# Ranking by one key in fp16 parts, weight maxima on TensorE, and four row buffers for the plain sums, in a one-core graph network kernel

## The reference

```python
h = jnp.maximum(_layernorm(x), 0.0)
x = x + gat_conv(relu(gat_conv(h, W1, ...)), W2, ...)   # layers 1, 2: attention over edges
h = jnp.maximum(_layernorm(x), 0.0)
x = x + gcn_conv(relu(gcn_conv(h, W3, ...)), W4, ...)   # layers 3, 4: plain normalised sums
```

## Time and profile before

| | |
|---|---|
| median of 3 runs | 2283.92 us (2281.28 to 2285.07) |
| the profiled execution | 2278.45 us, of which its span is 2276.7 us |
| busy, share of the span | PE 97%, PEld 63%, DVE 67%, ACT 41%, POOL 40% |
| mean granted clock of TensorE | 0.992 |
| DMA | 407.32 MB, 179 GB/s |

### The profile page before, as it was taken

How to read it: one execution, slowest core, us unless ns; L and a number is a source line. 1 busy time by engine, 2 the same in 40 slices (tenths; PEclk the granted TensorE clock), 3 DMA queues, 4 the chain that set the end, 5 groups by cost and what they waited for, 6 DMA issues and landing times.

```text
span 2276.7 us, 36746 instructions
## 1 busy us (share of the span) xinstructions
PE 2212.1 (97%) x13888; PEld 1428.2 (63%) x13888; DVE 1520.7 (67%) x3352; ACT 935.1 (41%) x1291; POOL 904.6 (40%) x1071
## 2 busy tenths in 40 slices
PE   6999999999999999999999999999999999999997
PEld 3666666666666666666666666666665666666664
DVE  6888885444577776334589999766555657885564
ACT  3333433333455445433454444433333333333442
...
GB/s 141 154 118 106 111 112 113 113 127 202 160 195 190 186 188 167 124 167 119 192 209 184 195 207 207 200 250 241 244 241 205 222 185 237 247 252 178 181 208 82
DMA packets 125668, 407.32 MB, mean 179 GB/s; under 512 B 21993, under 2 KB 22151, under 8 KB 125364
## 3 DMA queue, kind: packets, MB, share of 16 engines
...
## 4 chain that ended last, share of the span: by engine, by line
PE 80%; DVE 8%; POOL 4%; issue 4%; DMA 2%; ACT 2%; SPq 0%; POOLq 0%; ACTq 0%; DVEq 0%
PE ps_h L893 67%; PE ps_z L876 8%; DMA edge_mem<-rows,pos_dst 2%; PE ps_e L960 1%; PE ps_e L961 1%; DVE z_lo L1106 1%; DVE bn L1054 1%; POOL out L604 1%; DVE edge_mem L1136 1%; DVE res L1125 1%; ACT row_out L782 1%; POOL edge_mem L599 1%; DVE res L1115 1%; POOL rstd L613 1%; PE ps_e L968 0%
## 5 line engine op out<-in xcount | busy, mean ns | idle before, releaser
L893 PE MATMUL ps_h<-w_hi,z_hi 128*128 128x384 f16 x3792 | 928.4, 327 | 0.4 <-DVE w_lo L1045 0.4
L893 PE MATMUL ps_h<-w_lo,z_hi 128*128 128x384 f16 x3792 | 928.2, 327 | 0.0
L893 PE MATMUL ps_h<-w_hi,z_lo 128*128 128x384 f16 x3792 | 927.9, 326 | 0.0
L1106 DVE TENSOR_TENSOR z_lo<-ps_z,z_hi 128x768 f16<-128x768 f32 x316 | 301.7, 955 | 484.5 <-ACT z_hi L787 483.8
L893 PEld LDWEIGHTS ps_h<-w_lo,z_hi 128*128 128x128 f16 x3792 | 371.5, 98 | 246.4 <-issue 1.9
L893 PEld LDWEIGHTS ps_h<-w_hi,z_lo 128*128 128x128 f16 x3792 | 371.5, 98 | 246.0 <-issue 1.4
L893 PEld LDWEIGHTS ps_h<-w_hi,z_hi 128*128 128x128 f16 x3792 | 371.3, 98 | 223.6 <-issue 19.9
L782 ACT ACTIVATE row_out<-ps_h,grow 128x768 f32<-128x768 f32 x237 | 212.9, 898 | 637.7 <-PE ps_h L893 628.1
L876 PE MATMUL ps_z<-ident,z 128*128 128x128 f32 x1896 | 261.0, 274 | 24.8 <-ACT z L795 23.6
L611 POOL TENSOR_SCALAR veps<-mv 128x1 f32<-128x1 f32 x158 | 87.5, 554 | 457.2 <-DVE mv L1057 441.9
L787 ACT ACTIVATE z_hi<-ps_z 128x768 f16<-128x768 f32 x316 | 253.8, 803 | 15.4 <-PE ps_z L876 15.4
...
## 6 DMA issues: line engine op xcount, KB each, us to landing
...
```

The source lines that it names most:

```text
L893: last = nc.tensor.matmul(ps_h[s][:, a, 0:HALF], zp[s][:, c, :], wp[:, c, a * HALF:(a + 1) * HALF], start=(c == 0 and zp is z_hi and wp is ...
L1106: V.tensor_tensor(pair3(z_lo[t.slot]), psum_pair(ps_z), pair3(z_hi[t.slot]), ALU.subtract).then_inc(z_lo_ready, 1)
```

## The change

It touches five places.

- **Ranking by one key.** `row_key` holds (dst - NP/2) * 2560 + index, so that one compare with a sum (`is_lt`) per column takes the place of two passes over 128x2560. The one-hots and `sorts` are f16, and `sorts` holds four parts of 7 bits (dst low, dst high, src low, src high) of which `keep_ranks` makes the numbers again. A column stands in two of every three windows.
- **Weight maxima.** `all_max` is a TensorE product of ones with a diagonal of the maxima, and DVE takes the maximum of the row. For W1 it stands in window 0, for W2 to W4 in `side_step(0)` of the windows in `max_at`. The load of W1 is issued one window later, behind the load of the second tile's rows; DVE takes W1's maxima behind the second tile's statistics, and makes scale and lower halves of W1 ahead of the third tile's statistics.
- **Masks' rows.** The dst values are turned by one transpose behind `prefixes`, stored (`store_dst`) and loaded back to all 128 partitions by one broadcast DMA of 2 x 2560 values (`load_masks`). `mask_diag` and `mask_rows` are gone, and `mask_make` has two instructions for four.
- **Side products moved.** `prefixes`, `turn_positions` and `turn_meta` stand in `side_step(0)` of a later window; the DVE work between them is spread over more windows; the clearing product at the head of layer 2 is gone; `sqrt_degree` stands in layer 2.
- **Plain sums.** Layers 3 and 4 share `sum_rows`, `sum_carry` and `sum_mm` with four row buffers, filled three sums ahead; the first four are gathered in two windows. `plain_at` and `last_at` begin later and end at the same window as before.

```diff
-    RANKED = 2 + 2 * ET
-    ORDER = RANKED + 4
-    SCATTERED = ORDER + 20
-    ORDERED = SCATTERED + 4
-    EACH = -(-NT // 20)
+    assert NP * EP <= 2 ** 25
+    rank_at = {2 + (3 * c) // 2: c for c in range(EC)}
+    RANKED = max(rank_at) + 2
+    COUNTED = RANKED + 1
+    TURNED = COUNTED + 4
+    ORDER = TURNED + 4
+    EACH = 4
+    SCATTERED = ORDER + -(-NT // EACH)
+    ORDERED = SCATTERED + 5
+    MASKS = ORDER + 3
+    assert ORDERED + 8 < NT
...
-    plain_at = {begin["4"] + 2 + (8 * j) // 5: j for j in range(ET)}
-    last_at = {begin["5"] + 3 + (7 * j) // 5: j for j in range(ET)}
+    plain_at = {begin["4"] + 4 + (3 * j) // 2: j for j in range(ET)}
+    last_at = {begin["5"] + 4 + (27 * j) // 20: j for j in range(ET)}
...
+    max_at = {2: TURNED + 4, 3: ORDERED + 1, 4: begin["2m"] + 14}
...
+            def store_dst():
+                sp.wait_ge(dst_turned, 1)
+                sp.dma_start(dst_rows, rows_t[0:2 * ET, :]).then_inc(dst_stored, 16)
+            def load_masks():
+                sp.wait_ge(dst_stored, 16)
+                sp.dma_start(rank_mem[:, 0:2, :].rearrange("p a q -> p (a q)"),
+                             bass.AP(dst_rows.tensor, dst_rows.offset, [[0, P], [1, 2 * EP]])).then_inc(masks_loaded, 16)
...
-                if w == -3:
+                if w == -2:
...
+                if w == COUNTED + 1:
+                    store_dst()
+                if w == COUNTED + 3:
+                    load_masks()
+                if w == TURNED + 2:
...
+            def sum_rows(layer, j):
+                h = j + (layer - 1) * ET
                 if j >= 4:
-                    pool.wait_ge(edge_done, 3 * ET + 2 + (j - 3))
-                gather(last_src[j % 4], pos_src[:, j:j + 1], table[4][0:NP - PURE * P, :], last_in[j % 4])
-                gather(last_base[j % 4], pos_base[:, j:j + 1], base_rows, last_in[j % 4])
-            def first_last_rows():
+                    pool.wait_ge(edge_done, h - 1)
+                gather(last_src[j % 4], pos_src[:, j:j + 1], table[layer][0:NP - PURE * P, :], last_in[j % 4])
+                if layer == 3:
+                    gather(last_base[j % 4][:, 0:D], pos_dst[:, j:j + 1], table[3][0:NP - PURE * P, :], last_in[j % 4])
+                else:
+                    gather(last_base[j % 4], pos_base[:, j:j + 1], base_rows, last_in[j % 4])
...
+                for layer, at in ((3, plain_at), (4, last_at)):
+                    if w in at and 4 <= at[w] + 3 < ET:
+                        sum_rows(layer, at[w] + 3)
+                    for k in range(2):
+                        if w == min(at) - 2 + k:
+                            if k == 0:
+                                (plain_rows_free if layer == 3 else last_rows_free)()
+                            sum_rows(layer, 2 * k)
+                            sum_rows(layer, 2 * k + 1)
...
-            def all_max(layer):
-                pool.wait_ge(w_max, layer)
-                nc.gpsimd.partition_all_reduce(w_scale[:, layer - 1, 1:2], w_scale[:, layer - 1, 0:1], P, RMAX).then_inc(w_max_all, 1)
...
-                if w == ORDERED + 3:
+                if w == begin["2"] + 2:
...
-            def mask_rows(j):
-                pe.wait_ge(dst_diag, j + 1)
-                nc.tensor.matmul(mask_ps, ones[:, :], diag2[:, :, :].rearrange("p a q -> p (a q)"),
-                                 start=True, stop=True, skip_group_check=True).then_inc(mask_mm, 1)
...
+                    if k == 0:
+                        if w == COUNTED:
+                            prefixes()
+                        if w == TURNED:
+                            turn_positions()
+                        if w == ORDERED - 1:
+                            turn_meta()
+                        for layer, at in max_at.items():
+                            if w == at:
+                                all_max(layer)
...
-                if 2 <= w < RANKED and w % 2 == 1:
-                    rank_mm((w - 2) // 2)
+                if w - 1 in rank_at:
+                    rank_mm(rank_at[w - 1])
...
+            def all_max(layer):
+                pe.wait_ge(w_max, layer)
+                nc.tensor.matmul(w_max_ps, ones[:, :], w_diag, start=True, stop=True, skip_group_check=True).then_inc(w_max_all, 1)
...
-                if w == RANKED:
-                    prefixes()
-                if w == RANKED + 2:
-                    turn_positions()
-                if w == ORDERED:
-                    turn_meta()
-                if w == begin["2"]:
-                    clear_for_edges()
+                if w == 0:
+                    all_max(1)
...
-                    V.tensor_reduce(w_scale[:, layer - 1, 0:1], w_top[:, layer - 1, :], AX_X, ALU.max).then_inc(w_max, 1)
+                    step(V.tensor_reduce(w_scale[:, layer - 1, 0:1], w_top[:, layer - 1, :], AX_X, ALU.max))
+                    V.tensor_scalar(w_diag, ident[:, :], w_scale[:, layer - 1, 0:1], None, ALU.mult).then_inc(w_max, 1)
...
+                step(V.tensor_reduce(sc[:, 1:2], w_max_ps, AX_X, ALU.max))
...
-                V.scalar_tensor_tensor(row_cmp, row_iota, edge_id[:, col], row_dst, ALU.is_lt, ALU.subtract).then_inc(ranks_step, 1)
+                k = c * 4
+                V.tensor_scalar(row_cmp, row_key, e_f[:, 2, col], 0.0, ALU.is_lt, ALU.add, accum_out=e_rank[:, 0, 0:1]).then_inc(ranks_step, 1)
...
-                V.tensor_scalar(row_cmp, row_cmp, e_f[:, 2, col], 0.0, ALU.is_gt, ALU.add, accum_out=e_rank[:, 0, 0:1]).then_inc(ranks_step, 1)
...
-                V.tensor_scalar(sorts[:, slot, 0:ET], iota_c[:, 0:ET], e_rank[:, 1, 0:1], e_f[:, 0, col], ALU.is_equal, ALU.mult)
-                V.tensor_scalar(sorts[:, slot, ET:2 * ET], iota_c[:, 0:ET], e_rank[:, 1, 0:1], e_f[:, 1, col], ALU.is_equal, ALU.mult)
+                for n in range(4):
+                    V.tensor_scalar(sorts[:, slot, n * ET:(n + 1) * ET], iota_c[:, 0:ET], e_rank[:, 1, 0:1], e_f[:, 3 + n, col],
+                                    ALU.is_equal, ALU.mult)
...
-                V.tensor_scalar(e_arg[:, :], mask_ps[:, 0:P], dst_of[:, col], FAR, ALU.is_equal, ALU.mult).then_inc(mask_part, 1)
-                V.tensor_scalar(same_t[:, j, :], mask_ps[:, P:2 * P], dst_in[:, col], None, ALU.is_equal)
-                dve.wait_ge(mask_part, j + 1)
-                V.tensor_scalar(far_mask[:, j, :], e_arg[:, :], -FAR, None, ALU.add).then_inc(mask_ready, 1)
+                if j == 0:
+                    dve.wait_ge(masks_loaded, 16)
+                V.tensor_scalar(far_mask[:, j, :], far_mask[:, j, :], dst_of[:, col], -FAR, ALU.not_equal, ALU.mult)
+                V.tensor_scalar(same_t[:, j, :], same_t[:, j, :], dst_in[:, col], None, ALU.is_equal).then_inc(mask_ready, 1)
...
+                step(V.tensor_scalar(row_key, row_cmp.bitcast(I32), -float(NP // 2), float(EP), ALU.add, ALU.mult))
+                V.tensor_tensor(row_key, row_key, row_iota, ALU.add)
...
+                if w == -1:
+                    scale_w(1)
+                    for c in range(KC):
+                        low_w(1, c)
...
-                if w == RANKED + 1:
+                if w == COUNTED + 1:
+                    first_sums()
+                if w == COUNTED + 2:
+                    other_sums()
+                if w == COUNTED + 3:
                     node_positions()
-                if w == RANKED + 2:
-                    last_edges()
-                if w == RANKED + 3:
+                if w == TURNED + 1:
+                    keep_positions()
+                    last_edges(0, ET // 2)
+                if w == TURNED + 2:
+                    last_edges(ET // 2, ET)
```

192 lines of the change are left out of this document (84 added, 108 removed).

## The result

The changed kernel takes 2227.19 us (median of 4 executions, 2225.99 to 2231.59) beside 2284.49 us before (4 executions, 2281.28 to 2285.30): ratio 0.9755, 95% interval 0.9738 to 0.9772. The profiled executions are 2225.99 and 2278.45 us, with spans of 2224.1 and 2276.7 us. So the profiled pair differs by 52.5 us and the medians by 57.3.

A forecast was written before the change was run, and what follows sets the result against it. TensorE's work plus its waits was taken to bound the kernel. The terms summed to 47.7 us, 46.2 after 1.5 for new waits, giving 2232 from the profile or 2238 from the median; predicted 2237 us, range 2229 to 2251.

The forecast's parts named there:

- W2's reduction: Window of W2's maxima: TensorE's wait for z and matmuls at half clock behind it all go, 6.3 us.
- no column outgrew its window: Rival on DVE's ranking: columns too long to hide under TensorE; 16.5 us lost at 7.7 us each, 2254; chance 0.02.
- four buffers did help: Rival on layer 3's plain sums: four buffers do not help, all 9.2 us of waits stay, 2245 us; chance 0.12.
- the power at its new place: Rival: the moved power over the degrees holds up layer 2's edges, 6 to 12 us, 2246 us; chance 0.05.
- The clock's rival: Each new short wait brings a stretch at 1.2 GHz; three or four cost 6 to 8 us, 2244; chance 0.10.
- Two of my signs: Signs expected in the profile: `rank_mm` at 0.2 to 0.3 us a column; TensorE's carried-row waits under 3 us.
- plain sums of layer 3: 7.5 (bounds 4 and 9.2): Rows asked three sums ahead, not one, remove TensorE's carried-row waits: 7.5 us of 9.2, leaving 1.7.
- The offset of 5.5 us: Median of before lies 5.5 us above its profiled execution; 2232 from the profile, 2238 from the median.
- Products of a column: Ranking's products on TensorE, f16 with 198 columns: 0.63 to 0.23 us, twenty times, 8.0 us (bounds 5.0 and 11.0).
- The start: First product at 18.1 us instead of 28.94, less a 1.6 us wait and 0.8 for clock: 8.4 (bounds 6.5 and 9.2).
- Waits for z: 3.4: Two waits behind a busy GpSimd, the degrees' power and eight gathers in one window: 3.4 us (bounds 0 and 3.7).
- new short waits: Allowance for short new waits in denser windows: 1.5 us put back, taking the sum from 47.7 to 46.2 us.

The follow-up runs named there:

- run 2: Changed kernel with the rows of layer 3's plain sums asked one sum ahead instead of three, four buffers kept: 2246.29 us.
- run 7: Changed kernel with layer 3's plain sums 1.6 windows apart as before, instead of 1.5, rows still asked three sums ahead: 2226.81 us.
- run 3: Changed kernel with the four weight maxima reduced across partitions on GpSimd instead of TensorE: 2241.43 us.
- run 1: The kernel before, unchanged, profiled a second time: 2284.23 us, ratio to before 1.0001.
- run 9: The changed kernel, unchanged, profiled again: 2226.17 us, ratio 0.9748.
- run 4: Changed kernel with the ranking's one-hots and sorted values in f32 instead of f16: 2236.72 us.
- run 6: Changed kernel with the power over the degrees (`sqrt_degree`) back in layer 1: 2227.31 us.
- run 12: Changed kernel with carried-row copy ahead of z, norm factors ahead of gathers, and edge-weight transposes behind the next turn: 2224.71 us.
- run 14: Changed kernel with W3's load one piece a window, carried-row copy ahead of z, and norm factors ahead of gathers: 2223.77 us, ratio 0.9733.
- run 10: Changed kernel with ACT's copy of a sum's carried row ahead of its window's z instead of behind it: 2225.92 us.

## Why the prediction was wrong

**The bound and the mechanisms were right.** TensorE's work plus its waits is the time, and every edit acted where I had put it: DVE's column 5.20 us for 5.25, W2's reduction 6.3 us, the end of the ranking 4.6 for 4.5, the masks' products 8.7 for 8.6 ahead of new waits, the clearing 1.7 for 1.8, the first product at 17.5 for 18.1. The 6.3 us are those of the first profile; the second has 5.2 there. None of the rivals came: no column outgrew its window, four buffers did help (runs 2 and 7), the granted clock was 1.00 from 22 us to the last tiles, the power at its new place cost nothing. The clock's rival took each short wait for a stretch at 1.2 GHz; the three waits of 1.0 to 1.1 us in the last sums left the clock at 1.00. What the rule of the Trainium skill, VectorE: DVE Perf Modes, section Rules for kernel authors (reduce across partitions on GpSimd), would have kept, run 3 measured as 14.2 us slower. Two of my signs did not hold: `rank_mm` takes 0.1 us a column where I had 0.2 to 0.3, and the waits for the carried row are 3.3 us, over the 3 I allowed, in layer 4 and not in layer 3.

**The step that failed is the term "plain sums of layer 3: 7.5 (bounds 4 and 9.2)".** I took the sum of idle times in the earlier trace rows as all that the waits could give back. By turns the same seven waits are 11.0 us in that profile and 14.4 in the second (run 1). A wait costs its idle time and about 0.25 us to get going again (runs 1 and 2), and where the clock falls behind it 1.9 us in all (run 1). I also left 1.7 us of waits, as layer 4 had; none came. The term is 3.5 us too small in the first pair of profiles and 7.1 in the second (14.6), and its upper bound was no bound. It alone takes the time out of the range: my upper bounds add up to 53.5 us, the first pair gained 52.8 and the second 57.6, with 5.4 us above the bound in the plain sums and 1.6 at the start.

**The offset of 5.5 us between the profiled execution and the median of before was carried over as a constant.** The second profile shows what it is made of: of 5.2 us that it is longer, 3.5 are the plain sums' waits and 1.8 a wait in the last sums, and both places lost their waits for gathers or z by the change. That is the difference between 52.5 and 57.3 us. Not all that varies is gone: 10 executions of run 1 spread over 8.4 us and 5 of run 9 over 2.2, but the four of the changed kernel in the result over 5.6. By it I went from 2232 to 2238, where the changed kernel's median lies only 1.2 us above its profile.

**Products of a column: 9.9 for 8.0.** Run 4 shows that the format gives 0.5 us a column. I had 198 columns in mind; `sorts` is twice as wide now, so there are 238. At the f16 pitch that is 0.10 us, and the measured 0.135 leaves nearly nothing for the three loads, which I had taken half into the sum.

**The start: 9.8 for 8.4.** The first product came 0.6 us earlier than I had it, and the wait for the third tile's z was 0.6 us, not 1.6. The 0.8 us for the clock were due: the first tile's products took 7.5 us (17.53 to 25.04), where before they took 6.5 (28.94 to 35.47), since 3.1 us of them ran at half clock and 1.4 before. The first profile was a lucky one in this: where half clock lasted to 23.5 us or longer (runs 4, 6, 12 and 14) they took 8.6 to 8.7 us. So it is in part luck that the measured 9.8 lies near 8.4.

**Waits for z: 3.4.** The second of them lay in the last sums (2.77 us at 2059.50, behind eight gathers in one window), as I said, but what came in its place, three waits of 1.1 us with their restarts (4.0 us by turns), I had only in the 1.5 us for new short waits. Runs 10 and 14 show whose they are: ACT's copy stands behind a z that is late behind GpSimd's gathers. Together with 0.75 us in the masks' stretch the new waits came to 4.7 us for my 1.5, and hid part of the larger misses.

**What stays open.** The start differs by up to 1.6 us from profile to profile in the same order. Two parts of it can be read: the first product (17.5 to 18.6 us) follows the end of DVE's six maxima (12.95 to 13.96 us) by 4.6 to 4.7 us each time, and half clock ends anywhere from 20.6 to 24.4 us. Why either varies is open. Open too is what `load_meta` costs where it stands on SP's queue, and how much of the late turns near 395 us W3's load makes.
